# Group norm, channel norm, 1x1 projection and gate on one core: the clamp of the variance and the last product of the factor go to GpSimd, and the tiny scalar chain takes another instruction form

## The reference

```python
y  = (x - mean_g) / sqrt(var_g + 1e-5)       # _gn: 32 groups of 4 channels, over all pixels
u  = mean(y, axis=channel)                   # per pixel, over the 128 channels
s  = sqrt(var(y, axis=channel, ddof=1))
n  = (y - u) / (s + 1e-6)
out = x + y * (einsum('bchw,oc->bohw', n, W) + b)
```

## Time and profile before

| | |
|---|---|
| median of 3 runs | 1963.65 us (1959.81 to 1964.78) |
| the profiled execution: its own time | 1956.86 us |
| its span | 1955.1 us |
| granted TensorE clock, mean | 0.992 |
| busy share of the span | PE 89%, DVE 92%, ACT 74%, POOL 74% |
| DMA | 670.84 MB, mean 343 GB/s |

### The profile page before, as it was taken

The page is one execution under the profiler, slowest core; times in us unless marked ns, Lnnn a source line. Parts: engine busy times, 40 slices in busy tenths (PEclk is TensorE's granted clock), DMA queues, the critical chain, the costliest instruction groups (busy, mean ns, idle before and its releaser), DMA issues.

```text
span 1955.1 us, 55325 instructions
## 1 busy us (share of the span) xinstructions
PE 1738.8 (89%) x22562; PEld 986.7 (50%) x22562; DVE 1797.6 (92%) x2120; ACT 1438.8 (74%) x2498; POOL 1453.9 (74%) x1684
## 2 busy tenths in 40 slices
PE   0079998999899998999989999899988999899998
PEld 0055554555455554555545555555545555455554
DVE  5669999999899998999989999999989999998887
ACT  5598885888768885788858888588866888544442
POOL 0077877878778886788768787787877888788885
PEclk9989999999999999999999999999999999999999
DMA  9989998999999998999989999899998999844775
GB/s 379 390 311 341 375 377 305 398 374 375 333 313 403 359 387 322 336 392 371 384 307 384 375 379 356 308 409 374 374 333 321 391 362 385 321 192 188 268 253 221
DMA packets 184140, 670.84 MB, mean 343 GB/s; under 512 B 20688, under 2 KB 21072, under 8 KB 183888
## 3 DMA queue, kind: packets, MB, share of 16 engines
q1 hardware_dynamic: 110160, 398.85, 55.3%
q10 hardware_dynamic: 73728, 268.47, 34.6%
HBM read 398.80 MB, written 268.44 MB: 341 GB/s over the span
## 4 chain that ended last, share of the span: by engine, by line
PE 48%; DVE 27%; issue 9%; DMA 9%; POOL 2%; ACT 2%; SPq 2%; POOLq 0%; ACTq 0%; DVEq 0%
PE proj_ps L733 27%; PE sums_ps L722 12%; DVE scaled L632 9%; PE factor_ps L708 9%; DMA tiles<-x 6%; DVE tiles L645 5%; DVE bn L676 4%; DVE bn L677 4%; DMA out<-tiles 3%; SPq L408 2%; POOL tiles L441 1%; DVE var L651 1%; POOL tiles L452 1%; ACT unused L509 1%; DVE gn L580 1%
## 5 line engine op out<-in xcount | busy, mean ns | idle before, releaser
L733 PE MATMUL proj_ps<-scaled,w_t 128*128 128x512 f32 x2048 | 997.5, 610 | 0.2 <-DVE scaled L632 0.2
L452 POOL TENSOR_SCALAR tiles<-tiles,out_shift 128x1024 f32<-128x1024 f32 x512 | 573.9, 1121 | 233.8 <-DVE tiles L645 218.9
L645 DVE SCALAR_TENSOR_TENSOR tiles<-proj_ps,gate_shift,tiles 128x1024 f32<-128x1024 f32 x512 | 642.8, 1255 | 46.7 <-PE proj_ps L733 46.3
L441 POOL TENSOR_SCALAR tiles<-tiles,norm_scalars 128x1024 f32<-128x1024 f32 x512 | 615.8, 1203 | 58.0 <-DMA tiles<-x 57.0
L509 ACT ACTIVATE unused<-tiles,bn 128x1024 uint8<-128x1024 f32 x560 | 634.9, 1134 | 2.0 <-issue 1.7
L632 DVE TENSOR_TENSOR scaled<-tiles,factor_ps 128x1024 f32<-128x1024 f32 x512 | 618.1, 1207 | 8.7 <-PE factor_ps L708 8.0
L524 ACT ACTIVATE squares<-tiles 128x1024 f32<-128x1024 f32 x512 | 537.5, 1050 | 100.5 <-POOL tiles L441 71.9
L733 PEld LDWEIGHTS proj_ps<-scaled,w_t 128*128 128x128 f32 x2048 | 351.9, 192 | 248.5 <-issue 247.5
L708 PE MATMUL factor_ps<-pieces,pick_sb 128*128 128x128 bf16 x4096 | 319.7, 221 | 104.3 <-DVE scaled L632 89.8
L722 PEld LDWEIGHTS sums_ps<-tiles,const_sb 128*32 128x32 f32 x8192 | 193.7, 109 | 397.9 <-issue 263.6
L722 PE MATMUL sums_ps<-tiles,const_sb 128*32 128x128 f32 x8192 | 332.0, 280 | 12.2 <-ACT squares L524 12.2
(11 more groups left out here) (56 smaller groups left out, 672.5 us busy)
## 6 DMA issues: line engine op xcount, KB each, us to landing
tiles<-x SPq DMA_DIRECT2D x760, 512.0 KB, 9.4
out<-tiles ACTq DMA_DIRECT2D x512, 512.0 KB, 6.7
const_sb<-const SPq DMA_DIRECT2D x1, 193.5 KB, 2.3
scaled<-w SPq DMA_DIRECT2D x1, 64.0 KB, 2.1
scaled<-ident SPq DMA_DIRECT2D x1, 64.0 KB, 2.1
pick_sb<-pick SPq DMA_DIRECT2D x1, 8.0 KB, 2.2
bias_sb<-bias SPq DMA_DIRECT2D x1, 0.5 KB, 2.2
```

The costliest lines, as they stand in the source:

```text
L441: nc.gpsimd.tensor_scalar(place(s), place(s), norm_scalars[:, 0:1], norm_scalars[:, 1:2], ALU.add, ALU.mult).then_inc(normed, 1)
L452: nc.gpsimd.tensor_scalar(place(s), place(s), 1.0, out_shift[:, 0:1], ALU.mult, ALU.add).then_inc(finished, 1)
L645: nc.vector.scalar_tensor_tensor(out=place(s), in0=proj_ps[:, s % 2, :], scalar=gate_shift[:, 0:1], in1=place(s), op0=ALU.add, op1=ALU.mul ...
L733: mm = nc.tensor.matmul(proj_ps[:, s % 2, h:h + BANK], w_t[:, :], scaled[:, s % 2, h:h + BANK], start=True, stop=True)
```

## The change

Three edits. The clamp of the variance goes from DVE (behind L651) to POOL (behind `finish`). The last product of the factor goes from DVE at phase 2 to POOL at phase 1; as one instruction with a scalar and two tensors it becomes two there, a shift by -2 and a product. The scalar chain of `gn_scalars` uses `tensor_scalar` with both operands as one-column scalars, in place of `scalar_tensor_tensor`.

```diff
@@ pool
                 nc.gpsimd.tensor_tensor(miss[:, :], miss[:, :], approx[:, :], ALU.mult).then_inc(miss_squared, 1)
+                pool.wait_ge(miss_squared, done)
+                nc.gpsimd.tensor_scalar(miss[:, :], miss[:, :], 1.0, -2.0, ALU.mult, ALU.add).then_inc(miss_shifted, 1)
+                pool.wait_ge(miss_shifted, done)
+                nc.gpsimd.tensor_tensor(factor[:, :], miss[:, :], approx[:, :], ALU.mult).then_inc(factor_done, 1)
+
+            def clamp(done):
+
+                pool.wait_ge(var_sum_done, done)
+                nc.gpsimd.tensor_scalar(var[:, :], var[:, :], TINY, 1.0 / (P - 1), ALU.max, ALU.mult).then_inc(var_done, 1)
...
                     if (s := behind(step, LAG_OUT, own, before)) is not None:
                         finish(b, step, s, before)
+                    if var_of is not None:
+                        clamp(var_of)
                     if fit_of is not None:
                         split_second(fit_of, step)
@@ vector, gn_scalars
-                    then(nc.vector.scalar_tensor_tensor(out=cell(5), in0=cell(4), scalar=cell(4), in1=cell(1),
-                                                        op0=ALU.mult, op1=ALU.add))
...
+                    then(nc.vector.tensor_scalar(cell(5), cell(4), cell(4), cell(1), ALU.mult, ALU.add))
...
-                    then(nc.vector.scalar_tensor_tensor(out=cell(7), in0=cell(7), scalar=cell(7), in1=cell(5),
-                                                        op0=ALU.mult, op1=ALU.subtract))
+                    then(nc.vector.tensor_scalar(cell(7), cell(7), cell(7), cell(5), ALU.mult, ALU.subtract))
...
-                    then(nc.vector.scalar_tensor_tensor(out=cell(11), in0=cell(8), scalar=cell(10), in1=cell(9),
-                                                        op0=ALU.mult, op1=ALU.add))
+                    then(nc.vector.tensor_scalar(cell(11), cell(8), cell(10), cell(9), ALU.mult, ALU.add))
@@ vector, period
-                        dve.wait_ge(var_sum_done, ready)
-                        nc.vector.tensor_scalar(var[:, :], var[:, :], TINY, 1.0 / (P - 1), ALU.max, ALU.mult)\
-                            .then_inc(var_done, 1)
...
-                    if (ready := set_behind(step, LAG_FIT, b, own, before)) is not None:
-
-                        dve.wait_ge(miss_squared, ready)
-                        nc.vector.scalar_tensor_tensor(out=factor[:, :], in0=miss[:, :], scalar=-2.0, in1=approx[:, :],
-                                                       op0=ALU.add, op1=ALU.mult).then_inc(factor_done, 1)
```

More of the change, by code:

```diff
@@ L301, in norm_gate_kernel @@
         miss_squared = sem("miss_squared")
+        miss_shifted = sem("miss_shifted")
         factor_done = sem("factor_done")
@@ L475, in period @@
                 for step in steps(own, before, nxt):
+                    var_of = set_behind(step, LAG_VAR, b, own, before)
                     root_of = set_behind(step, LAG_ROOT, b, own, before)
@@ L585, in gn_scalars @@
                     then(nc.vector.tensor_scalar(cell(4), cell(0), pivot_of(of), None, ALU.subtract))
-                    then(nc.vector.scalar_tensor_tensor(out=cell(5), in0=cell(4), scalar=cell(4), in1=cell(1),
-                                                        op0=ALU.mult, op1=ALU.add))
-                    then(nc.vector.scalar_tensor_tensor(out=cell(4), in0=cell(4), scalar=bn_part, in1=cell(2),
-                                                        op0=ALU.mult, op1=ALU.subtract))
-                    then(nc.vector.scalar_tensor_tensor(out=cell(5), in0=cell(5), scalar=bn_part, in1=cell(3),
-                                                        op0=ALU.mult, op1=ALU.add))
-                    then(nc.vector.scalar_tensor_tensor(out=cell(5), in0=cell(4), scalar=cell(4), in1=cell(5),
-                                                        op0=ALU.mult, op1=ALU.subtract))
+                    then(nc.vector.tensor_scalar(cell(5), cell(4), cell(4), cell(1), ALU.mult, ALU.add))
+                    then(nc.vector.tensor_scalar(cell(4), cell(4), bn_part, cell(2), ALU.mult, ALU.subtract))
+                    then(nc.vector.tensor_scalar(cell(5), cell(5), bn_part, cell(3), ALU.mult, ALU.add))
+                    then(nc.vector.tensor_scalar(cell(5), cell(4), cell(4), cell(5), ALU.mult, ALU.subtract))
                     then(nc.vector.tensor_scalar(cell(6), cell(4), pivot_of(of), None, ALU.add))
```

## The result

The changed kernel takes 2001.68 us in the median of 4 runs (1996.09 to 2005.7), against 1963.23 us for the kernel before in the same comparison: ratio 1.0202, 95% interval 1.0186 to 1.0218. The forecast was 1963 us and no change, with a range up to 1979. The time lies far above it. The profiled execution took 1999.69 us against 1956.86, so there are 42.8 us to explain (38.5 us between the medians).

What follows compares the result with a forecast made beforehand. The prediction took PE to bound the kernel, with 116 us of waits to win; its terms, -17.9 - 4.2 + 2.5 + 25.6 + 1.5 - 8.4, summed to -0.9 us, about 1963 us, range 1946 to 1979.

Steps and rivals of the forecast that it cites:

- the clamp on POOL: Clamp behind POOL's finish: 303 ns, bounds 187 and 456; covered in plain sets, +2.5 us where norms wait for DMA.
- the cover: Reciprocal on DVE starts at about the same time despite the root 0.2 us later; without this, 0.2 us per set.
- What bounds the kernel: PE never has slack; its 116 us of waits are all that a change in the steady part can win.
- The clamp leaves DVE: Scale at phase 1 no longer waits for the clamp, -17.9 us; at step 0 in 6 batches, -4.2 us.
- The product on POOL: Shift and product make POOL's pieces 0.76 us later, so PE stops at phase 3: +25.6 us; last batch +1.5 us.
- The scalar chain: New instruction form in the group statistics saves 1.2 us a batch, 7 times: -8.4 us, bounds 0 and -10.7.
- In the last batch, and in plain sets, nothing is lost: Clamp covered in plain sets; last batch keeps 0.14 of 0.90 us slack, losing only two stops, +1.5 us.
- The waits: PE's waits for the scale fall from 89.8 to about 50 us, for pieces rise from 14.3 to about 45 or 50.
- My two signs of being wrong: PE's waits for pieces staying below 20 us, or POOL's waits for DMA growing by more than 20 us.
- The slower one, DMA: Rival: POOL's later finish delays stores and loads, so norms wait longer for DMA; 16 us reach PE, 1979 us; chance 0.20.
- the scalars gain nothing: Rival: the new scalar form waits behind POOL as the old one did; +8.4 us, 1971 us; chance 0.05.
- DVE as the bound: Rival: DVE limits the kernel, so all time taken off it goes; -142 us, 1821 us; chance 0.02.

Runs made afterwards that it cites:

- e1: Changed kernel with the clamp on POOL as a multiplication and an addition of 0, maximum left out: 1965.08 us, ratio 1.0028.
- e11: Changed kernel with the clamp on POOL as multiply then add 0, maximum left out, and the product back on DVE: 1939.17 us, ratio 0.9885.
- e4: Changed kernel with clamp and product both back on DVE, so only the scalar chain differs from the kernel before: 1952.72 us, ratio 0.9951.
- e5: Kernel before with the new scalar chain, the variance written to PSUM and the clamp on DVE reading it there: 1931.47 us, ratio 0.986.
- e2: Changed kernel with the clamp back on DVE, shift and product still on POOL: 1972.28 us, ratio 1.0053.
- e6: Changed kernel, one execution, six forms of the clamp on POOL in turn by set: mult then add 298 ns, mult alone 531 ns.
- e9: Changed kernel, one execution, six further clamp forms on POOL in turn by set, including a copy; subtract then mult took 652 ns.

## Why the prediction was wrong

The step that failed is one term, **the clamp on POOL**. I interpolated its 303 ns between the copy and the finish, and called 456 ns, the two-input product, the upper bound. The finish is one of the cheap forms, which among those tried are the pairs of multiplications and additions: the clamp measured 638 ns, outside my bounds, and 0.82 us of POOL's time with the gaps on either side. From that the rest follows by the forecast's own mechanism. I had named the cover that would go: the reciprocal was to start at the same time, because the root would be 0.2 us late and the scale out of its way. In the set shown, counted from the start of the finish, the root became 0.65 us late and the reciprocal 0.40, and the cover was too short. A second thing has no term in the sum at all: behind the long stops at the end of the batches PE's matmuls ran at the lower clock, some 10 us in the profiled execution. Removing only the error in the clamp's operations (e1) gives a ratio of 1.0028, 5.6 us above before, where the sum said -0.9. Most of what is left between the two is again the clamp's move, which at 298 ns gained 13 us (e11 against e4) where the forecast had -22.1 + 2.5 = -19.6.

The others, point by point:

- *What bounds the kernel*: right. DVE lost 144 us of busy time and nothing came of it; PE's waits were the budget.
- *The clamp leaves DVE* (-22.1 us): right in kind. The 0.28 us went, in the changed kernel and in e5 and e11; the move from e4 to e5 measured 18 us, to e11 13 us.
- *The product on POOL* (+25.6 us): right. Without the dear clamp PE's stop for the pieces idles 0.57 us at phase 3, where the forecast had 0.6 for the second set of a pair. Measured: 20 us with the clamp on DVE (e2 against e4), 28 us with the cheap clamp on POOL (e1 against e11). Shift and product took 298 and 459 ns, forecast 0.30 and 0.46. The finish of phase 1 came 0.78 us later in its chain, which is also what the forecast's own terms add up to; it wrote 0.76. I kept the row's 456 ns and not the 0.28 us estimated from the Trainium skill, page "GPSIMD Engine Reference", section "Elementwise — side-by-side cycle accounting"; the product's measured 459 ns decides for the row.
- *The scalar chain* (-8.4 us): right. The new form takes 272 to 274 ns in the median, at most 277 in any trace, where the old took up to 1.07 us; e4 measures 0.49%, 10 us, with an interval of 6 to 13. The others of the chain were not all short, as I had read: a `tensor_scalar` over two columns took 169 to 1099 ns before (L584) and takes 169 to 1109 ns in the changed kernel (L597).
- *In the last batch, and in plain sets, nothing is lost*: wrong, by the same error (13.68 us a set instead of 13.34). In the last batch, of the 0.90 us of slack I had left 0.14, and the clamp took that and 0.34 us more in each set.
- *The waits*: the pieces were to rise to 45 to 50 us and rose to 62.8; the scale was to fall to 50 and fell to 67.1. My two signs of being wrong, pieces below 20 us or waits for DMA 20 us up, both stayed away: they watched the rivals and not the price that failed.
- *The rivals*: none was it. The slower one, DMA, is refuted, since POOL's waits for DMA fell; that the scalars gain nothing is refuted by e4, and DVE as the bound by its 144 us. I had seen the right sort of mechanism, a cover gone, and priced it at 0.2 us per set, but made no rival of it, because my bounds excluded it.

## What to carry to other kernels

The duration of an elementwise instruction on POOL depends on which operations it applies; a price is to be taken from a row with the same operations, not only the same shape, and where there is none the upper bound has to lie well above the nearest row. Work taken off the busiest engine pays only if what takes its place comes early enough for the next instruction in that engine's own order: here DVE stood idle in front of the scale that PE was waiting for. Before moving an instruction away because it is long, ask whether it is long or held up: the clamp's own work on DVE was 0.23 to 0.29 us, and reading its input from PSUM brought it back to that.

## What the runs showed of the hardware that I had not expected

- On POOL, on 128x128 float32 in SBUF: mult-add, add-mult and mult-mult 297 to 298 ns, a copy 290 ns, a multiplication, an addition or a maximum alone 529 to 546 ns, and every other pair tried (with max, min or subtract) 642 to 659 ns (638 ns in the changed kernel).
- The forms with a maximum or minimum stand alone on POOL, with 0.08 to 0.10 us free before and behind (e6, e9, the changed kernel). All others, the dear 652 ns of subtract then mult included, overlap their neighbours by about 0.02 us.
- Two moves that cost 20 and 21 us alone cost 49 us together, and most of the excess is in PE's busy time, not in its waits.
- Behind stops of 2.90 and 2.49 us (at 1009.38 and 1020.26 in the trace of the changed kernel) the projection matmuls took 3.58 and 3.20 us instead of 1.94, with a mean granted clock of 0.58 over the 4 us from the spread on, in both places.
